# Moving three of eight shared product groups from the tail of a decoder layer into its expert rounds

## The reference, cut to what matters

```python
gu = x @ se_gate_up_w.T                                             # shared expert, 1408 wide
shared = silu(gu[:, :1408]) * gu[:, 1408:] @ se_down_w.T
shared = shared * sigmoid(x @ shared_gate_w.T)
weights, sel = top_k(softmax(x @ gate_w.T), 4)                      # 60 experts, 4 for a token
for w13_e, w2_e, cw_e in experts:                                   # sparse
    gu_e = x @ w13_e.T
    acc = acc + cw_e[:, None] * ((silu(gu_e[:, :352]) * gu_e[:, 352:]) @ w2_e.T)
return x_residual + shared + acc
```

## Time and profile before

| | us |
|---|---|
| median of 3 runs | 1175.94 (1175.72 to 1178.64) |
| the profiled execution | 1178.55 |
| its span, first to last instruction | 1176.8 |
| PE busy | 1087.5 (92%) |
| rounds, about | 715 to 1101 |
| shared second products and gathers | 1101 to 1176.8 |

### The profile page before, as it was taken

The page is one execution under the profiler, slowest core; times in us unless marked ns, Lnnn a source line. Parts: engine busy times, 40 slices in busy tenths (PEclk is TensorE's granted clock), DMA queues, the critical chain, the costliest instruction groups (busy, mean ns, idle before and its releaser), DMA issues.

```text
span 1176.8 us, 18687 instructions
## 1 busy us (share of the span) xinstructions
PE 1087.5 (92%) x5538; PEld 588.5 (50%) x5538; DVE 502.1 (43%) x1385; ACT 263.9 (22%) x806; POOL 370.3 (31%) x843
## 2 busy tenths in 40 slices
PE   3999799999899989999889999999999979899797
PEld 1444465445554456544655555555545535444454
DVE  7843674339654395543846701222122111111144
ACT  0332232414332243333414010111111111111000
POOL 3575451855527563374200370000000000000272
PEclk9999899999999999999999999999999999999899
DMA  8999201000010000102013986999999999999753
GB/s 319 345 397 383 92 2 57 15 1 13 2 56 15 13 1 9 47 15 96 2 48 102 367 319 237 384 349 379 366 383 380 372 378 368 380 361 369 252 140 110
DMA packets 76584, 233.11 MB, mean 198 GB/s; under 512 B 11362, under 2 KB 13766, under 8 KB 68814
## 3 DMA queue, kind: packets, MB, share of 16 engines
q1 hardware_dynamic: 58830, 197.90, 46.9%
q10 hardware_dynamic: 11520, 20.98, 5.1%
q0 software_dynamic: 6144, 13.13, 3.6%
HBM read 178.75 MB, written 53.22 MB: 197 GB/s over the span
## 4 chain that ended last, share of the span: by engine, by line
PE 62%; SPq 14%; DVE 11%; DMA 7%; issue 5%; ACT 1%; DVEq 0%; ACTq 0%
PE ps L852 13%; PE ps L941 7%; PE ps L1146 6%; SPq L474 6%; PE ps L1229 6%; PE ps L1330 5%; PE ps L1225 5%; SPq L547 4%; PE ps L1261 3%; DMA arena<-in_se_down 3%; PE ps L1257 2%; DMA arena<-in_w 2%; PE ps L998 2%; PE ps L1203 2%; DMA arena<-in_x 2%
## 5 line engine op out<-in xcount | busy, mean ns | idle before, releaser
L852 PE MATMUL ps<-arena 128*100 128x512 f32 (+3 forms) x552 | 208.3, 524 | 4.3 <-ACT arena L1352 3.6
L786 POOL DMA_INDIRECT arena<-ys_d,slot_u x32 | 36.5, 1141 | 415.7 <-issue 412.5
L852 PEld LDWEIGHTS ps<-arena 128*100 128x100 f32 (+1 forms) x552 | 83.1, 173 | 94.9 <-issue 86.5
L1229 PE MATMUL ps<-arena 128*64 128x352 f32 x640 | 107.9, 494 | 16.6 <-issue 12.6
L2084 DVE COPY arena<-ps 128x512 f32<-128x512 f32 x40 | 27.7, 692 | 222.1 <-PE ps L1217 222.1
L941 PE MATMUL ps<-arena 128*100 128x512 f32 x256 | 114.1, 593 | 0.0
L1146 PE MATMUL ps<-arena 128*128 128x400 f32 x288 | 98.3, 501 | 2.2 <-DVE arena L2064 1.1
L1225 PE MATMUL ps<-arena 128*128 128x352 f32 x320 | 98.1, 459 | 0.8 <-issue 0.8
L1404 ACT ACTIVATE arena<-ps,arena 100x345 f32<-100x345 f32 x128 | 69.6, 547 | 107.8 <-DVE arena L1851 105.3
L1229 PEld LDWEIGHTS ps<-arena 128*64 128x64 f32 x640 | 48.9, 147 | 70.7 <-issue 60.4
L712 POOL TENSOR_TENSOR arena<-arena 115x512 f32<-115x512 f32 (+1 forms) x29 | 30.5, 1051 | 160.9 <-DVE arena L1777 125.1
(11 more groups left out here) (229 smaller groups left out, 1524.6 us busy)
## 6 DMA issues: line engine op xcount, KB each, us to landing
arena<-in_w SPq DMA_DIRECT2D x60, 1408.0 KB, 17.6
arena<-in_w SPq DMA_DIRECT2D x60, 512.0 KB, 17.6
xs_d<-zero SPq DMA_DIRECT2D x5, 3328.0 KB, 25.2
arena<-in_w SPq DMA_DIRECT2D x60, 192.0 KB, 19.8
arena<-xs_d ACTq DMA_DIRECT2D x40, 256.0 KB, 8.0
ys_d<-arena ACTq DMA_DIRECT2D x40, 256.0 KB, 8.8
ys_d<-zero SPq DMA_DIRECT2D x2, 3328.0 KB, 25.6
arena<-in_se_up SPq DMA_DIRECT2D x11, 512.0 KB, 6.7
```

The source lines that it names most:

```text
L852: last = nc.tensor.matmul(ps[0:m, k, 0:cols[1] - cols[0]], lhs(c), w[:, c, cols[0]:cols[1]], start=(c == 0), stop=(c == n_c - 1))
L1229: last = nc.tensor.matmul(ps[half * HALF:(half + 1) * HALF, 3 + gu, 0:I], xsT[1][:, c, half * HALF:(half + 1) * HALF], w13_s[s][1 + half][ ...
```

## The change

Three of the eight groups of the shared second products (first half of the tokens, output columns 0 to 383) are made ahead of rounds 10, 13 and 16, in bank 5 of PSUM, which is free after round 7. The down weights are loaded in four column parts of 128 columns, each with a semaphore of its own: the first three are issued by SP ahead of the refill that serves round 10, 13 and 16, the fourth behind the last refill. `dnT` moves to the place of the router's tables. The residual is no longer loaded when the last products are made but when the last results are stored, in four parts of two batches, and DVE waits for the part that it needs. PE, ACT and SP have their rounds from the eighth on written out in place of loops.

```diff
+ACC_PARTS = 4
+PART_ROUNDS = (10, 13, 16)
...
         acc = carve(B, D)
+        assert top[0] <= down_at + DC * 2 * I + 3 * D
+        top[0] = route_at
         dnT = carve(DC, 400)
...
-            with sp.Fori(0, ROUNDS // 2 - 2) as ii:
+            def load_down(d):
+
+                sp.wait_ge(sh_up, UNITS)
+                sp.dma_start(w_down[:, :, d * P:(d + 1) * P],
+                             se_down[:, d * P:(d + 1) * P].rearrange("(c p) n -> p c n", p=P)).then_inc(down_loaded[d], 16)
+
+            with sp.Fori(0, LATE) as ii:
                 for s in range(2):
                     refill(s, ii * 2 + s)
-            refill(0, ROUNDS - 4)
-            refill(1, ROUNDS - 3, True)
-
-            sp.wait_ge(sh_up, UNITS)
-            sp.dma_start(w_down, se_down.rearrange("(c p) n -> p c n", p=P)).then_inc(down_loaded, 16)
+            for i in range(2 * LATE, ROUNDS - 2):
+                if i + 2 in PART_ROUNDS:
+                    load_down(PART_ROUNDS.index(i + 2))
+                refill(i % 2, i, i == ROUNDS - 3)
+
+            for d in range(len(PART_ROUNDS), DC):
+                load_down(d)
             sp.wait_ge(y_full[0], ROUNDS)
-            sp.wait_ge(y_full[1], ROUNDS)
-            sp.dma_start(acc[0:S], x2_d.rearrange("b s d -> s b d")).then_inc(acc_loaded, 16)
+            for k in range(2):
+                sp.wait_ge(y_stored[k], 16 * ROUNDS + 1)
+            for n in range(ACC_PARTS):
+                own = slice(n * B // ACC_PARTS, (n + 1) * B // ACC_PARTS)
+                sp.dma_start(acc[0:S, own, :], x2_d[own].rearrange("b s d -> s b d")).then_inc(acc_loaded[n], 16)
...
-            with pe.Fori(LATE, ROUNDS // 2 - 1) as ii:
-                round_(0, ii * 2, ii, ii)
-                round_(1, ii * 2 + 1, ii, ii + 1)
+            def shared_part(n):
+
+                pe.wait_ge(down_loaded[n], 16)
+                pe.wait_ge(sh_h, UNITS)
+                if n:
+                    pe.wait_ge(dnT_copied, n)
+                for m in range(MC):
+                    last = nc.tensor.matmul(ps[:, 5, 0:400], w_down[:, m, n * P:(n + 1) * P], hT_all[:, m, 0:400],
+                                            start=(m == 0), stop=(m == MC - 1))
+                last.then_inc(dnT_full, 1)
+
+            for i in range(2 * LATE, ROUNDS - 2):
+                if i in PART_ROUNDS:
+                    shared_part(PART_ROUNDS.index(i))
+                round_(i % 2, i, i // 2, (i + 1) // 2)
...
-            pe.wait_ge(down_loaded, 16)
-            pe.wait_ge(sh_h, UNITS)
+            for n in range(DC):
+                pe.wait_ge(down_loaded[n], 16)
+            pe.wait_ge(dnT_copied, len(PART_ROUNDS))
...
             for half in range(2):
                 for d in range(DC):
+                    if half == 0 and d < len(PART_ROUNDS):
+                        continue
...
+            for i in range(2 * LATE, ROUNDS - 1):
+                if i in PART_ROUNDS:
+                    n = PART_ROUNDS.index(i)
+                    act.wait_ge(dnT_full, n + 1)
+                    nc.scalar.activation(dnT[:, n, :], ps[:, 5, 0:400], ACT.Copy).then_inc(dnT_copied, 1)
+                round_(i % 2, i, i <= ROUNDS - 4)
...
-            dve.wait_ge(acc_loaded, 16)
-
             def add_gathered(b):
+                dve.wait_ge(acc_loaded[b * ACC_PARTS // B], 16)
```

More of the change, by code:

```diff
@@ L265, in decoder_kernel @@
         xn3_end = top[0]
+        route_at = top[0]
         oh = carve(B, E)
@@ L269, in decoder_kernel @@
         slot_e = carve(B, E)
+        route_end = top[0]
         bts = carve(10, E)
@@ L288, in decoder_kernel @@
         acc = carve(B, D)
+        assert top[0] <= down_at + DC * 2 * I + 3 * D
+        top[0] = route_at
         dnT = carve(DC, 400)
+        assert top[0] <= route_end
         top[0] = xs_at
@@ L356, in decoder_kernel @@
         se_loaded = [sem(f"se_loaded{r}") for r in range(3)]
-        down_loaded = sem("down_loaded")
-        acc_loaded = sem("acc_loaded")
+        down_loaded = [sem(f"shared_down_loaded{d}") for d in range(DC)]
+        acc_loaded = [sem(f"residual_loaded{n}") for n in range(ACC_PARTS)]
         xn3_loaded = sem("xn3_loaded")
```

## The result

The change makes the kernel slower. Medians of 20 runs each on the same chip: 1181.86 us after (1176.49 to 1186.12), 1176.55 us before (1169.75 to 1188.77); the ratio is 1.005, with a 95% interval of 1.0032 to 1.0068. That is 5.9 us more by the ratio, where 4.0 less were forecast. The profiled execution took 1185.78 us, its span is 1184.0.

A forecast was written before the change was run, and what follows sets the result against it. PE was taken to bound the early rounds, DMA those from round 12, PE the tail by 7 us over the gathers. Terms -7.0 - 1.5 + 7.9 - 4.4 + 1.0 = -4.0 us gave 1171.9 us, range 1167.0 to 1178.5.

The forecast's parts named there:

- The loops written out cost nothing: Rounds: writing out the loops adds 0 us, since the rounds before 870 us are written out and keep PE busy.
- -7.0 and -1.5, the tail without DVE's waits for PE: Tail: DVE's last wait for PE goes (-7.0 us), and its earlier wait that held POOL's gather goes (-1.5 us).
- The groups are covered: Rounds: the three moved groups, 22.1 us of PE, are hidden beside seven rounds with 23.9 us to spare.
- rival 5: Rounds: the groups are not covered, part of their 22.1 us stays; with one group +3.4 us, 1179.3; chance 0.06.
- +7.9, the parts: Rounds: three down-weight part loads delay later weights, 2.64 us each at 30 ns per 512-byte packet, +7.9 us.
- Rival 1: Rounds: small packets choke the full queue, 24 us at 91 ns, giving 1188; decides from 45 ns on; chance 0.10.
- rival 2: Rounds: the part loads are hidden because the DMA engines have room; the +7.9 falls away, 1164; chance 0.08.
- rival 3: Rounds: 512-byte packets move as fast per byte as large ones; -6.1 us in all, 1169.8; chance 0.10.
- -4.4 + 1.0, store and residual: Tail: first gather 4.5 us after the last store's issue, not 8.9 (-4.4 us); residual beside the gathers costs +1.0.
- rival 4: Tail: store keeps its own 5.7 us, or residual costs all 4.4 us, or both: -1.2 to +2.2, 1176; chance 0.20.
- PE's idle time after round 19: Sign at the start of the tail: PE should go on after round 19 with less than 1 us of idle.
- The warning: Sign for round 19: it should begin near 1096 us; the forecast is wrong if it begins over 4 us away.

The follow-up runs named there:

- f4: The kernel before, with half of each large weight loaded for rounds 10 to 19 and loops written out on PE, SP and ACT: ratio 0.9775 to before.
- e9: The changed kernel with rounds 8 to 17 back in loops, the groups behind a test, the middle one at round 14: ratio 0.9997 to before.
- e4: The kernel before with only rounds 8 to 17 written out on PE, SP and ACT: ratio 1.0058 to before.
- e6: The kernel before with rounds 8 to 17 written out on PE alone: ratio 1.0033 to before.
- g1: The kernel before, with POOL raising an unused semaphore 224 times in each of nine rounds, written out straight: ratio 1.0139 to before.
- e2: The changed kernel with the residual's four loads issued as early as in the kernel before: ratio 1.0034 to before.
- e3: The changed kernel with down parts contiguous in memory and the residual issued early: ratio 1.0014 to before.
- e8: The changed kernel with contiguous down parts, early residual and rounds back in loops, the middle group at round 14: ratio 0.9939 to before.
- e11: The changed kernel with contiguous parts, early residual, loops, middle group at round 14, but without the first three parts' loads: ratio 0.9910 to before.
- e7: The kernel before with rounds 8 to 17 written out on SP and ACT alone: ratio 1.0009 to before.
- e1: The changed kernel with each down part contiguous in memory, 5632 bytes per partition, so no 512-byte packets: ratio 1.0015 to before.
- e12: The changed kernel with contiguous down parts and rounds in loops, the middle group at round 14, residual still behind the last store: ratio 0.9953 to before.
- f3: The kernel before, with half of each large weight loaded for rounds 10 to 19, SP and ACT written out, PE looped: ratio 0.9779 to before.
- g2: The kernel before, with POOL raising an unused semaphore 224 times in each of nine rounds, in a loop: ratio 0.9998 to before.
- f1: The kernel before with seven extra 16 KB transfers issued from POOL during the rounds: ratio 1.0024 to before.

## Why the prediction was wrong

The step that failed is "The loops written out cost nothing: the rounds before 870 are written out already and keep PE busy without a gap". The observation was right, and it didn't bear on the question. PE indeed shows no gap at a block (f4). The blocks take the DMA engines, and the rounds before 870 have the lead to hide that (q8 moves five blocks from 725 to 870 us in the kernel before, and PE doesn't wait), while the rounds from 12 on have none. The step should have been a term: 0 was put, and e9 against the change gives 6.2 us, e4 alone 6.8, e6 3.9.

The Trainium skill (Runtime: NRT & Kernel Launch, Instruction fetch mechanics) says that each engine's sequencer fetches its program in 16 KiB blocks by a DMA queue of its own, and calls the cost of a block "mostly hidden". The 16 KB packets of q8 agree with the first for PE; POOL's blocks in g1 were packets of 8 KB, all on q14, and there the measurement decides. The second holds in f4 and fails in e4, e6 and g1, where the transfers that bound the kernel need the same DMA engines. The same section says that kernels prefer full unrolling; here the loop with its tests is 0.53% to 0.75% faster, and the measurement decides.

The other steps, in the order of the sum:

- *-7.0 and -1.5, the tail without DVE's waits for PE.* Held. With the early residual, where these two terms stand alone, the tail is 80.0, 78.4, 80.2 and 78.0 us (e2, e3, e8, e11): 79.2 in the mean, against 87.6 of the five kernels with the tail as it was (before, e4 to e7). That is 8.4 for 8.5.
- *The groups are covered.* Held (e11); rival 5 is out.
- *+7.9, the parts.* Right in kind, 1 to 2 us too small. Between 880 and 1106 us a packet of 512 bytes took 36.8 ns in the mean in the change and 33.8 in e9 (worked out from the trace), where 30 was taken: 9.7 and 8.9 us of 16 engines for the three parts. The times agree, less sharply: e9 against e11, which lacks the loads, is 0.87% (10.2 us, 4.6 to either side), small packets against contiguous ones 4.1 us (e1) or 5.2 (e9 against e12). Rival 1 needed 45 ns. SP did stand as it says (9.7 to 18.8 us behind a part), but in e9 too (11.2, 17.2 and 18.3 us), with rounds as short as those of e8. So it is out as the main cause, and so are rival 2 (no cost) and rival 3 (22 ns).
- *-4.4 + 1.0, store and residual.* The store landed in 2.0 us, within the forecast's 1.9 to 4.15, and the first gather came at 3.9 for the 4.5 expected. But the +1.0 should have stood near the upper bound of 4.4 that the prediction gave. From the last store to the fifth gather it is 13.2 us after, 13.6 in e12, 12.9 with the early residual of e8, and 14.8 in the kernel before. The four kernels with the late residual have tails of 78.1 us in the mean, 1.1 less than the four with the early one, and by the times late against early is +1.9 us (the change and e2), +0.1 (e1 and e3) and +1.6 (e12 and e8), none of them beyond the intervals. So the net is near nothing, -1.1 by the tails and not below 0 by the times, and not -3.4: the first half of rival 4 was wrong, its second half ("the residual beside the gathers costs all its 4.4") right.

With these corrections the sum is -7.0 - 1.5 + 7.9 + 6.2 = +5.6 us, or 1.1 less, against 5.9 measured. Without the loops' term it is -0.6 to -1.7, and e9 has -0.4. With contiguous loads as well (4.1 to 5.2 less) it is -4.7 to -6.9; e12 has -5.5 and e8 -7.2. The 6.2 and the 5.2 are themselves taken from e9, so these sums test the other terms and not the loops'; what speaks for the loops' term apart from them is e4, 6.8 us without any of the change.

Of what was to show it, four points held: the groups stood without idle time ahead, DVE no longer waited for PE at the end, the first gather came early, and the chain that ended last ran through POOL's gathers and DVE. PE's idle time after round 19 was 2.3 us and not under 1; f3 and f4, whose down weights had landed long before, have 2.2 and 2.1 there, so some 2 us would have stood there without any wait for weights. It costs nothing, since the gathers end later.

```profile
1119.52 15.02 PE L1363 MATMUL ps<-arena 128*128 128x400 f32 x44 [2.27 <-issue]
```

The warning was round 19: it began at 1105.5, over 9 us from the 1096 that was forecast, 5 of it from ahead of the rounds and 4.2 from within.

## What to carry to other kernels

Where the DMA engines are full, a program's own length is traffic: look at the instruction queues in the DMA view before and after writing a loop out, on any engine, also one that is idle. If a loop must carry a few special rounds, a test inside it can be cheaper than writing it out. And a transfer that is moved out of one stage's way has to be costed in the stage that it lands in, at its full bytes, if the first thing that this stage does is to read memory too.

## What was unexpected of the hardware

- POOL, off the path, slowed the kernel by 1.4% merely by running 2016 instructions straight (16 blocks of 8 KB from round 8 to round 19 in place of 2), and by nothing that can be told when it ran them in a loop (g1, g2).
- With room in the DMA engines PE fetched seven blocks of 16 KB in 184 us and lost less than 0.1 us in the rounds (f3, f4).
- One transfer of 16 KB in a single row was cut into 16 packets of 1 KB (f1: 112 such packets for 7 transfers); an instruction block stays one packet.
